# Ten instead of six low-rank merges in the last pair of a fused attention and FFN kernel, with weight parts staged in two more buffers

## The chip, the cores and the metric

The kernel runs on one core of one Trainium2 chip. Its time is the device time of one execution in microseconds (us), the median over runs of the same program: 644.33 us before the change (three runs, 643.79 to 645.38).

## The reference

Sixteen batches of 64 tokens with 1024 channels go through three residual stages. Cut to what matters:

```python
x = x + xattn(layernorm(x), ctx)      # fake_quant(x) @ fake_quant(ctx), ctx: (16, 1024, 1024)
x = x + attn(layernorm(x))            # qkv, rotary, causal softmax, 32 heads of 32, out projection
x = x + ffn(layernorm(x))

def ffn(x, W, bias, A, Bf, coeffs, scales):
    out = einsum('bsd,od->bso', x, W) + bias
    xa  = einsum('bsd,erd->ebsr', x, A)           # 16 adapters of rank 16
    return out + einsum('ebsr,eor,e->bso', xa, Bf, coeffs * scales)
```

Adapters are linear, so the kernel adds them into the weight once: W' = W.T + A.T @ (w * Bf), with the 16 adapters of rank 16 as one product of rank 256. All products are to be nearly as exact as in float32.

## The kernel before

Two batches make a pair of 128 token rows; there are eight pairs. The first two stages go pair by pair and leave each pair's rows in a scratch tensor in DRAM. The third stage (FFN) comes after all pairs, tile by tile of 128 rows, t = 0 to 7. A product in near float32 is three float16 products, high by high, high by low and low by high (`dense`, L1104 to L1106): ScalarE writes the high part of an operand and VectorE the low part, what is left after it.

The FFN's weight is built in 16 units of 128 x 512. For each unit u:

- `merge(u)` on PE: six matmuls of 128x512 into one of two PSUM banks (`cross` in the profile, L1281 to L1283). It waits for the sum of unit u-2, which frees its bank.
- `merged_sum(u)` on VectorE (L835): adds the bank to the unit of W.T, in place.
- `merged_high(u)` on ScalarE (L378), then `merged_low(u)` on VectorE (L840): the float16 parts, over weights of the attention stage that are no longer used.

Merges 0 to 7 lie among the matmuls of the last pair, 8 to 11 between that pair and the FFN, 12 to 15 in the first half of the FFN of tile 0. W.T arrives in five loads, into `raw` (units 0 to 3), `lnt` (4, 5) and the place `wt` over the query, key and value weights, which is free once the last pair has used them.

A tile of the FFN is: `stats3` (mean and reciprocal deviation on VectorE, 13 instructions, most of them of one element per row and each behind a wait for the one before), `apply3` (normalisation into `lnt`, L1018), `y_turn` (eight transposes on PE, L1095), `y_high` (ScalarE, L517), `y_low` (VectorE, L1030), two halves of 24 matmuls, and `y_evac` (L1039) into an output tile that `residual` (L1025) has filled with the input rows and the bias. SP loads the rows of tile t+2 when `residual(t)` is done (L650).

Every engine works through its own list in order, and waits on semaphores. There is no scheduler: order is what is written here, in tables such as `{5: [at(m, 0)]}`, which say behind which of the eight weight blocks of a product a step is issued. The names `merged_sum`, `merged_low`, `stats3` and so on stand in VectorE's list in `last_pair` and behind the loops.

Of the kernel before, what the change touches and what calls it, by code (L numbers as in the profile page):

```python
# [22 lines left out]
PAIRS = BATCH // 2  # L23
KC = DM // P
# [28 lines left out]
def build(nc, x, ctx_in, consts, consts16, scal, qkv_w, out_w, bias_rows, out_bias, ffn_wt, ffn_bias, lora_a, lora_b, lora_w, out):  # L53
# [6 lines left out]
    with es:  # L60
# [78 lines left out]
        wt_lnt = lnt[:, :].rearrange("p (u n) -> p u n", u=2)  # L139
        yn_h = [xn_h[:, :, :], q1v[:, 0:DM].rearrange("p (k t) -> p k t", k=KC)]  # L140
# [102 lines left out]
        def wt_unit(u):  # L243
            k, cols = merge_unit(u)
            if u < 4:
                return wt_early[:, u, :]
            return wt_lnt[:, u - 4, :] if u < 6 else wt[:, k, cols]

        wt_load = {0: 0, 4: 1, 6: 2, 8: 3, 12: 4}
# [31 lines left out]
        def _(act):  # L281
# [188 lines left out]
            def last_pair(i):  # L470
                for n in range(4):
                    lora_high(n)
                qk_evac(i, 0)
                qk_evac(i, 1)
                exponent(i, 0)
                exponent(i, 1)
                qk_evac(i, 2)
                p_evac(i, 0)
                p_evac(i, 1)
                qk_evac(i, 3)  # L480
                v_evac(i, 0)
                exponent(i, 2)
                exponent(i, 3)
                c_high(i, 0)
                p_evac(i, 2)
                v_evac(i, 1)
                p_evac(i, 3)
                c_high(i, 1)
                for u in range(6):
                    merged_high(u)  # L490
# [29 lines left out]
            for u in range(6, 2 * KC):  # L520
                merged_high(u)
# [7 lines left out]
        def _(sp):  # L529
# [85 lines left out]
            def load_wt(n):  # L615
                ks = (slice(0, 4), slice(4, 6), slice(6, 8), slice(0, 4), slice(4, 8))[n]
                cols = slice(0, NT) if n < 3 else slice(NT, DM)
                sp.dma_start((wt_early, wt_lnt)[n] if n < 2 else wt[:, ks, cols], wt_v[:, ks, cols]).then_inc(s_wt[n], 16)
# [11 lines left out]
            load_wt(1)  # L630
            sp.wait_ge(s_qkv, 6 * PAIRS)
            load_wt(2)
# [3 lines left out]
            load_wt(3)  # L636
# [49 lines left out]
        def _(dve):  # L686
# [144 lines left out]
            def merged_sum(u):  # L831
                dve.wait_ge(s_wf, u + 1)
                if u in wt_load:
                    dve.wait_ge(s_wt[wt_load[u]], 16)
                dve.scalar_tensor_tensor(wt_unit(u), X[u % 2][:, :], 1.0 / (WSC * WSC), wt_unit(u), ALU.mult, ALU.add).then_inc(s_wsum, 1)  # L835
# [94 lines left out]
            def last_pair(i):  # L930
                lora_weights()
                for n in range(4):
                    lora_low(n)
                rotate(i, 0)
                out_base(i)
                rotate(i, 1)
                merged_sum(0)
                merged_sum(1)
                softmax_in(i, 0)
                softmax_in(i, 1)  # L940
                rotate(i, 2)
                softmax_out(i, 0)
                softmax_out(i, 1)
                rotate(i, 3)
                merged_sum(2)
                merged_sum(3)
                softmax_in(i, 2)
                softmax_in(i, 3)
                merged_sum(4)
                softmax_out(i, 2)  # L950
                softmax_out(i, 3)
                merged_sum(5)
                c_low(i, 0)
                c_low(i, 1)

# [92 lines left out]
            merged_sum(6)  # L1048
            merged_sum(7)
            out_evac(PAIRS - 1, 0)  # L1050
            merged_low(6)
            merged_low(7)
            merged_sum(8)
            y_low(0, 0)
            merged_sum(9)
            merged_low(8)
            out_evac(PAIRS - 1, 1)
            merged(10, 11)
            residual(0, 0, 0)
            merged(12)  # L1060
            stats3(1, 0)
            merged(13, 14, 15)
            merged_low(2 * KC - 1)
            apply3(1, 1)
# [25 lines left out]
        def _(pe):  # L1090
# [287 lines left out]
            def next_pair(i, ahead):  # L1378
# [10 lines left out]
                def codes_turned(e):  # L1389
                    if ahead:  # L1390
# [4 lines left out]
                qkv(i, 1, {0: [at(c, 0)], 2: [at(c, 1)], 4: [at(codes_turned, 0), at(qk_turn, i, 0)], 5: [at(c, 2), at(m, 0)], 7: [at(c, 3)]})  # L1395
                qkv(i, 2, {1: [at(c, 4)], 3: [at(codes_turned, 1), at(qk_turn, i, 1)], 4: [at(c, 5), at(m, 1)], 6: [at(scores, i, 0)], 7: [at(c, 6)]})
                qkv(i, 3, {1: [at(c, 7)], 2: [at(m, 2)], 5: [at(turned, i, 0), at(qk_turn, i, 2)], 6: [at(turned, i, 2), at(p_turn, i, 0)], 7: [at(p_turn, i, 1)]})
                qkv(i, 4, {1: [at(m, 3)], 4: [at(evacuated, i, 1), at(qk_turn, i, 3)], 6: [at(c, 8)], 7: [at(c, 9)]})
                qkv(i, 5, {0: [at(scores, i, 1)], 1: [at(c, 10, 11), at(m, 4)], 2: [at(c, 12, 13), at(m, 5)], 3: [at(c, 14, 15), at(values_due, i, 0)], 4: [at(values, i, 0)],
                           6: [at(evacuated, i, 0), at(p_turn, i, 2)], 7: [at(p_turn, i, 3)]})  # L1400
                project(i, 0, 0, {2: [at(values_due, i, 1)], 3: [at(values, i, 1)]})
                project(i, 1, 0)
                if ahead:
                    x_turn(i + 1)
                else:
                    merge(6)
                    merge(7)
# [23 lines left out]
            for u in range(8, 12):  # L1431
                merge(u)

            def ffn(t, s, n, first=False):
# [8 lines left out]
                if first and n == 1:  # L1443
                    between = {4: [at(y_turn, 1)]}
# [65 lines left out]
```

## Time and profile before

| | |
|---|---|
| median of three runs | 644.33 us |
| the profiled execution | 645.53 us |
| its span | 643.9 us |
| PE busy | 604.1 us, 94% of the span |
| VectorE (DVE) busy | 448.6 us, 70% |
| ScalarE (ACT) busy | 297.6 us, 46% |
| DRAM traffic over the span | 169 GB/s |
| mean granted clock of PE | 0.986 of full |

The profile is of one execution. Its times count from the start of the span; what lies around the span is 1.6 us. PE is the matmul engine, DVE is VectorE, ACT is ScalarE, SPq the queue of transfers. A matmul is pipelined: the duration in its row runs past the start of the next one, so the rate is read from the starts.

### The profile page before, as it was taken

Reading aid. Unit: us, or ns where it says so; the run is one execution under the profiler, and the core shown is the slowest. Engines: PE = TensorE matmul, PEld = TensorE weight load, DVE = VectorE, ACT = ScalarE, POOL = GpSimd, SP = SyncE. Lnnn points to the kernel's source line nnn. Section 1 sums busy time; section 2 is a strip of 40 time slices with the busy share of each in tenths; the row PEclk is TensorE's granted clock in tenths of the full one; section 3 lists DMA queues with packets and bytes.
Section 4 is the critical chain, followed back from the end, with each engine's and each line's share of the span. In section 5 each row is a group of like instructions: output and inputs, shape, how many; then the busy total and the mean of one; then the engine's idle time right before and its main releaser. Section 6 shows DMA issues by size and latency. Waiting matters only on the chain.

```text
span 643.9 us, 12627 instructions
## 1 busy us (share of the span) xinstructions
PE 604.1 (94%) x4832; PEld 299.6 (47%) x4832; DVE 448.6 (70%) x897; ACT 297.6 (46%) x374; POOL 11.1 (2%) x20
## 2 busy tenths in 40 slices
PE   1669987999999999999999999999999999899997
PEld 0234442454545555554445455544544554354453
DVE  7599995779747854885586568537865569767661
ACT  5888765774455545545634554555331233101010
POOL 3000000000000000000000000000000000000000
PEclk9879999999999999999999999999999999899999
DMA  9999896862284156317712751463240062023221
GB/s 320 385 388 383 331 301 235 280 227 70 98 263 164 67 195 213 115 65 259 258 69 84 251 186 65 168 219 103 98 163 2 1 212 97 35 78 119 84 79 49
DMA packets 38878, 109.17 MB, mean 170 GB/s; under 512 B 4026, under 2 KB 4282, under 8 KB 38848
## 3 DMA queue, kind: packets, MB, share of 16 engines
q1 hardware_dynamic: 37072, 104.35, 46.3%
q0 software_dynamic: 1344, 4.23, 1.7%
q8 instruction: 20, 0.33, 0.2%
q10 hardware_dynamic: 432, 0.18, 0.1%
q14 instruction: 10, 0.08, 0.0%
HBM read 100.35 MB, written 8.39 MB: 169 GB/s over the span
## 4 chain that ended last, share of the span: by engine, by line
PE 81%; DVE 11%; DMA 3%; SPq 2%; ACT 1%; issue 1%; DVEq 0%; ACTq 0%
PE dense L1104 16%; PE dense L1106 15%; PE dense L1105 15%; PE cross L1141 7%; PE turn L1095 6%; DVE wq L774 4%; PE dense L1235 4%; PE dense L1236 4%; PE dense L1237 4%; PE score L1198 2%; SPq L532 2%; DMA wq<-in_ctx 2%; PE score L1222 2%; DMA lnt<-in_ctx 1%; PE dense L1117 1%
## 5 line engine op out<-in xcount | busy, mean ns | idle before, releaser
L1104 PE MATMUL dense<-wq,xn_h 128*128 128x512 f16 x400 | 152.4, 381 | 0.0
L1105 PE MATMUL dense<-wq,xn_h 128*128 128x512 f16 x400 | 151.9, 380 | 0.0
L1106 PE MATMUL dense<-wq,xn_l 128*128 128x512 f16 x400 | 151.9, 380 | 0.0
L318 ACT ACTIVATE code<-raw,cst,qc 128x1024 uint8<-128x1024 f32 x74 | 90.2, 1237 | 17.9 <-DMA raw<-in_ctx 17.1
L1141 PE MATMUL cross<-code,q1t 128*128 128x512 f16 x256 | 74.7, 393 | 8.5 <-ACT code L318 4.2
L1106 PEld LDWEIGHTS dense<-wq,xn_l 128*128 128x128 f16 x400 | 39.2, 98 | 47.5 <-issue 0.6
L1104 PEld LDWEIGHTS dense<-wq,xn_h 128*128 128x128 f16 x400 | 39.2, 98 | 40.8 <-issue 2.8
L1105 PEld LDWEIGHTS dense<-wq,xn_h 128*128 128x128 f16 x400 | 39.3, 98 | 37.8 <-issue 0.9
L334 ACT ACTIVATE at<-turn 128x512 f32<-128x512 f32 x32 | 19.1, 597 | 76.8 <-PE turn L1095 76.0
L318 ACT ACTIVATE code<-lnt,cst,qc 128x1024 uint8<-128x1024 f32 x34 | 42.1, 1238 | 26.9 <-DMA lnt<-in_ctx 19.9
L803 DVE TENSOR_REDUCE smx<-score 128x8 f32<-128x512 f32 x32 | 22.0, 686 | 44.0 <-PE score L1198 44.0
L791 DVE TENSOR_TENSOR rope<-dense,cst 128x512 f32<-128x512 f32 x32 | 22.0, 689 | 39.0 <-PE dense L1106 22.3
L1141 PEld LDWEIGHTS cross<-code,q1t 128*128 128x128 f16 x256 | 23.6, 100 | 44.8 <-ACT code L318 10.3
L1235 PE MATMUL dense<-wo,rope 128*128 128x512 f16 x112 | 42.5, 380 | 0.0
L1236 PE MATMUL dense<-wo,rope 128*128 128x512 f16 x112 | 42.4, 379 | 0.0
L1237 PE MATMUL dense<-wo,rope 128*128 128x512 f16 x112 | 42.4, 379 | 0.0
L342 ACT ACTIVATE at<-at 128x512 f32<-128x512 f32 x32 | 20.0, 626 | 34.8 <-DVE at L806 34.8
L348 ACT ACTIVATE at<-turn 128x512 f32<-128x512 f32 x32 | 19.0, 595 | 19.4 <-PE turn L1095 19.4
L780 DVE SCALAR_TENSOR_TENSOR xa<-cross,qc,xa 64x1024 f32<-64x1024 f32 x16 | 20.4, 1273 | 8.1 <-PE cross L1141 7.9
L1095 PE MATMUL turn<-cst,lnt 128*128 128x128 f32 x128 | 17.6, 283 | 7.9 <-DVE lnt L761 5.4
L829 DVE SCALAR_TENSOR_TENSOR xb<-dense,xb 128x512 f32<-128x512 f32 x16 | 11.0, 690 | 20.0 <-PE dense L1237 18.0
L1104 PE MATMUL dense<-wq,q1t 128*128 128x512 f16 x64 | 24.3, 379 | 0.0
(159 smaller groups left out, 935.8 us busy)
## 6 DMA issues: line engine op xcount, KB each, us to landing
raw<-in_ctx SPq DMA_DIRECT2D x74, 512.0 KB, 4.8
lnt<-in_ctx SPq DMA_DIRECT2D x34, 512.0 KB, 4.3
wo<-in_ctx SPq DMA_DIRECT2D x12, 512.0 KB, 9.1
wo<-in_qkv_w SPq DMA_DIRECT2D x12, 512.0 KB, 12.3
wq<-in_ctx SPq DMA_DIRECT2D x8, 512.0 KB, 11.5
wq<-in_qkv_w SPq DMA_DIRECT2D x8, 512.0 KB, 12.1
x_scratch<-xb SPq DMA_DIRECT2D x8, 512.0 KB, 3.2
wq<-x_scratch SPq DMA_DIRECT2D x8, 512.0 KB, 3.7
```

The source lines that it names most:

```text
L318: act.activation(low_bytes, src, ACT.Identity, scale=qc[:, 1:2], bias=z2).then_inc(s_u8, 1)
L774: dve.scalar_tensor_tensor(lo, staged(j), WSC, hi, ALU.mult, ALU.subtract).then_inc(s_wlo, 1)
L791: dve.tensor_tensor(t1, src, cosb, ALU.mult)
L803: link(dve.tensor_reduce(smx[:, g % 2, :], s3, AX.X, ALU.max))
L1095: ins = pe.transpose(bank[:, k * P:(k + 1) * P], src[:, c:c + P], ident)
L1104: pe.matmul(bank[:, :], a_h[:, k, :], w_hi, start=(k == 0 and not started), stop=False)
L1105: pe.matmul(bank[:, :], a_h[:, k, :], w_lo, start=False, stop=False)
L1106: ins = pe.matmul(bank[:, :], a_l[:, k, :], w_hi, start=False, stop=(k == KC - 1 and not last))
L1141: ins = pe.matmul(X[n][:, :], lhs, code[:, c % RING, n * NT:(n + 1) * NT], start=(kc == 0), stop=(kc == KC - 1))
L1235: pe.matmul(D[n][:, :], c_h[:, k, :], wo_h[:, k, cols], start=(k == 0), stop=False)
L1236: pe.matmul(D[n][:, :], c_h[:, k, :], wo_l[:, k, cols], start=False, stop=False)
L1237: ins = pe.matmul(D[n][:, :], c_l[:, k, :], wo_h[:, k, cols], start=False, stop=(k == KC - 1))
```

## The change

Merges 0 to 9 now lie in the last pair, 10 and 11 between it and the FFN, 12 to 15 as before. Units 6 and 7 of W.T are loaded into `xa` (the residual rows' buffer) and units 8 and 9 into the buffer of turned codes `q1t`, so both can arrive before the query, key and value weights are free; one load of six parts fills the rest. On VectorE the sums move up with their merges, the statistics and normalisation of the second tile go from between the sums to behind the last low part, and so do both residuals. On PE the second tile's transposes move from behind block 4 to behind block 7, the last, of the second half of tile 0.

```diff
+        wt_xa = xa[:, :].rearrange("p (u n) -> p u n", u=2)
+        wt_q1t = q1v.bitcast(F32).rearrange("p (u n) -> p u n", u=2)
...
-            return wt_lnt[:, u - 4, :] if u < 6 else wt[:, k, cols]
-        wt_load = {0: 0, 4: 1, 6: 2, 8: 3, 12: 4}
+            if u < 10:
+                return (wt_lnt, wt_xa, wt_q1t)[(u - 4) // 2][:, u % 2, :]
+            return wt[:, k, cols]
+        wt_load = {0: 0, 4: 1, 6: 2, 8: 3, 10: 4}
...
-                for u in range(6):
+                for u in range(10):
                     merged_high(u)
...
-                ks = (slice(0, 4), slice(4, 6), slice(6, 8), slice(0, 4), slice(4, 8))[n]
+                ks = (slice(0, 4), slice(4, 6), slice(6, 8), slice(0, 2), slice(2, 8))[n]
...
             load_wt(1)
+            load_wt(3)
+            sp.wait_ge(s_cp, PAIRS)
+            load_wt(2)
             sp.wait_ge(s_qkv, 6 * PAIRS)
-            load_wt(2)
             sp.wait_ge(s_st, 32)
             for n in range(2):
                 sp.dma_start(xs[n], x2_dram[n, :, :]).then_inc(s_x2[n], 16)
-            load_wt(3)
             load_wt(4)
...
                 rotate(i, 2)
+                merged_sum(2)
                 softmax_out(i, 0)
                 softmax_out(i, 1)
                 rotate(i, 3)
-                merged_sum(2)
                 merged_sum(3)
+                merged_sum(4)
+                merged_sum(5)
                 softmax_in(i, 2)
                 softmax_in(i, 3)
-                merged_sum(4)
+                merged_sum(6)
                 softmax_out(i, 2)
                 softmax_out(i, 3)
-                merged_sum(5)
+                merged_sum(7)
                 c_low(i, 0)
+                merged_sum(8)
                 c_low(i, 1)
+                merged_sum(9)
...
             apply3(0, 0)
-            merged_sum(6)
-            merged_sum(7)
+            merged_low(6)
             out_evac(PAIRS - 1, 0)
-            merged_low(6)
             merged_low(7)
-            merged_sum(8)
+            merged_low(8)
+            merged_low(9)
+            merged_sum(10)
             y_low(0, 0)
-            merged_sum(9)
-            merged_low(8)
+            merged_sum(11)
+            merged_low(10)
             out_evac(PAIRS - 1, 1)
-            merged(10, 11)
+            merged(12)
+            merged(13)
+            merged(14)
+            merged(15)
+            merged_low(2 * KC - 1)
+            stats3(1, 0)
+            apply3(1, 1)
             residual(0, 0, 0)
-            merged(12)
-            stats3(1, 0)
-            merged(13, 14, 15)
-            merged_low(2 * KC - 1)
-            apply3(1, 1)
             residual(1, 1, 0)
...
-                project(i, 0, 0, {2: [at(values_due, i, 1)], 3: [at(values, i, 1)]})
+                project(i, 0, 0, {0: [at(m, 8)], 2: [at(values_due, i, 1)], 3: [at(values, i, 1)]})
                 project(i, 1, 0)
...
-                    merge(6)
-                    merge(7)
+                    merge(9)
                 project(i, 0, 1)
                 project(i, 1, 1)
...
             y_turn(0)
-            for u in range(8, 12):
+            for u in range(10, 12):
                 merge(u)
...
-                    between = {4: [at(y_turn, 1)]}
+                    between = {7: [at(y_turn, 1)]}
```

What stands in a row now. VectorE at the end of the last pair, before: `lnt<-cross` is the sum of unit 5, `rope<-score` the low part of the attention result (`c_low`), `wq<-raw` low parts of weight units, `BN_STATS` the start of the first tile's statistics.

```order
L835 SCALAR_TENSOR_TENSOR lnt<-cross,lnt 128x512
L822 SCALAR_TENSOR_TENSOR rope<-score,rope 128x4x64 x4
L840 SCALAR_TENSOR_TENSOR wq<-raw,wq 128x512 x4
L697 BN_STATS st<-wq 128x6
L698 BN_STATS st<-wq 128x6
```

VectorE at the same place in the changed kernel: `xa<-cross` is the sum of unit 7, `q1t<-cross` are those of units 8 and 9.

```order
L840 SCALAR_TENSOR_TENSOR xa<-cross,xa 128x512
L827 SCALAR_TENSOR_TENSOR rope<-score,rope 128x4x64 x2
L840 SCALAR_TENSOR_TENSOR q1t<-cross,q1t 128x512
L827 SCALAR_TENSOR_TENSOR rope<-score,rope 128x4x64 x2
L840 SCALAR_TENSOR_TENSOR q1t<-cross,q1t 128x512
L845 SCALAR_TENSOR_TENSOR wq<-raw,wq 128x512 x4
L702 BN_STATS st<-wq 128x6
L703 BN_STATS st<-wq 128x6
```

A sum now stands between the two `c_low`, and one between the second of them and the first low part of a weight, where none was.

PE at the end of tile 0's FFN, before: `dense` are its matmuls, `turn<-cst,lnt` the second tile's transposes.

```order
L1106 MATMUL dense<-wq,xn_l 128x512
L1104 MATMUL dense<-wq,xn_h 128x512
L1105 MATMUL dense<-wq,xn_h 128x512
L1106 MATMUL dense<-wq,xn_l 128x512
L1095 MATMUL turn<-cst,lnt 128x128 x8
L1104 MATMUL dense<-wq,xn_h 128x512
L1105 MATMUL dense<-wq,xn_h 128x512
L1106 MATMUL dense<-wq,xn_l 128x512
```

PE there in the changed kernel: the `dense<-wq,q1t` behind the transposes are the second tile's own first matmuls.

```order
L1116 MATMUL dense<-wq,xn_l 128x512
L1114 MATMUL dense<-wq,xn_h 128x512
L1115 MATMUL dense<-wq,xn_h 128x512
L1116 MATMUL dense<-wq,xn_l 128x512
L1105 MATMUL turn<-cst,lnt 128x128 x8
L1114 MATMUL dense<-wq,q1t 128x512
L1115 MATMUL dense<-wq,q1t 128x512
L1116 MATMUL dense<-wq,q1t 128x512
```

The transposes had three weight blocks (nine matmuls) of tile 0 behind them and now have those of the second tile, which need the transposed rows.

VectorE around the second tile's statistics, before: `wq<-cross` is a sum, `wq<-wq` a low part, `xa<-wq` the first residual.

```order
L840 SCALAR_TENSOR_TENSOR wq<-wq 128x512
L1025 TENSOR_TENSOR xa<-wq 128x1024
L835 SCALAR_TENSOR_TENSOR wq<-cross,wq 128x512
L840 SCALAR_TENSOR_TENSOR wq<-wq 128x512
L697 BN_STATS st<-wq 128x6
L698 BN_STATS st<-wq 128x6
```

VectorE at the last sums in the changed kernel.

```order
L840 SCALAR_TENSOR_TENSOR wq<-cross,wq 128x512
L845 SCALAR_TENSOR_TENSOR wq<-wq 128x512
L840 SCALAR_TENSOR_TENSOR wq<-cross,wq 128x512
L845 SCALAR_TENSOR_TENSOR wq<-wq 128x512 x2
L702 BN_STATS st<-wq 128x6
L703 BN_STATS st<-wq 128x6
```

The statistics now come behind the last of the low parts, and the first residual behind the normalisation.

## Rows read from the trace of the kernel before

**Rows 1.** The page: busy time of engines, and granted clock in 40 slices.
```profile
PE 604.1 (94%) x4832; PEld 299.6 (47%) x4832; DVE 448.6 (70%) x897; ACT 297.6 (46%) x374; POOL 11.1 (2%) x20
...
PEclk9879999999999999999999999999999999899999
```

**Rows 2.** Stretches: window, length, busy us by engine, granted clock, DMA share, GB/s.
```profile
534.00:550.00 16.00, 13.57 (x66) 6.12 (x63) 14.34 (x32) 5.27 (x9) 0.00 (x0) 1.00 0.18 67
550.00:557.00 7.00, 6.27 (x22) 2.55 (x23) 6.28 (x10) 1.89 (x3) 0.00 (x0) 0.76 0.00 0
```

**Rows 3.** Waits of PE, 534 to 557 us: total, times, longest.
```profile
PE cross L1281 <- DVE wq L835: 3.2, 3, 2.2
```

**Rows 4.** Timeline of PE: start, duration, instruction, [idle before, releaser].
```profile
538.76 0.39 PE L1281 MATMUL cross<-code 128*128 128x512 f16 x1 [0.60 <-DVE wq L835]
...
540.55 0.39 PE L1281 MATMUL cross<-code 128*128 128x512 f16 x1 [0.33 <-DVE wq L835]
...
550.73 0.39 PE L1281 MATMUL cross<-code 128*128 128x512 f16 x1 [2.23 <-DVE wq L835]
...
551.17 0.60 PE L1283 MATMUL cross<-code 128*128 128x512 f16 x1
...
554.80 0.38 PE L1106 MATMUL dense<-wq,xn_l 128*128 128x512 f16 x1
```

**Rows 5.** Timeline of PE, around the transposes of the last stage's rows.
```profile
529.36 0.38 PE L1235 MATMUL dense<-wo,rope 128*128 128x512 f16 x1
...
534.53 1.04 PE L1095 MATMUL turn<-cst,lnt 128*128 128x128 f32 x8
...
559.55 1.04 PE L1095 MATMUL turn<-cst,lnt 128*128 128x128 f32 x8
...
562.36 0.38 PE L1104 MATMUL dense<-wq,q1t 128*128 128x512 f16 x1
```

**Rows 6.** Timeline of VectorE, then of PE, in the last pair's attention.
```profile
500.42 0.69 DVE L814 TENSOR_TENSOR at<-at,ssum 128x512 f32<-128x512 f32 x1
...
501.86 0.60 PE L1095 MATMUL turn<-cst,at 128*128 128x128 f32 x4
```

**Rows 7.** Timeline of VectorE, 524 to 566 us.
```profile
524.68 0.76 DVE L822 SCALAR_TENSOR_TENSOR rope<-score,rope 128x256 f16<-128x256 f32 x2 [5.08 <-ACT rope L354]
525.48 2.50 DVE L840 SCALAR_TENSOR_TENSOR wq<-raw,wq 128x512 f16<-128x512 f32 x4
...
532.93 0.81 DVE L1018 TENSOR_SCALAR lnt<-wq,mv,nw 128x1024 f32<-128x1024 f32 x1
...
546.35 0.69 DVE L697 BATCH_NORM_STATS2 st<-wq 128x6 f32<-128x512 f32 x1
...
549.98 0.69 DVE L835 SCALAR_TENSOR_TENSOR wq<-cross,wq 128x512 f32<-128x512 f32 x1
...
553.09 0.69 DVE L835 SCALAR_TENSOR_TENSOR wq<-cross,wq 128x512 f32<-128x512 f32 x1 [0.62 <-PE cross L1283]
...
555.09 0.81 DVE L1018 TENSOR_SCALAR lnt<-wq,mv,nw 128x1024 f32<-128x1024 f32 x1
555.81 1.22 DVE L1025 TENSOR_TENSOR outb<-wq 128x1024 f32<-128x1024 f32 x1
...
560.81 1.29 DVE L1030 TENSOR_TENSOR q1t<-turn,q1t 128x512 f16<-128x512 f32 x2 [3.19 <-ACT q1t L517]
562.02 0.68 DVE L697 BATCH_NORM_STATS2 st<-wq 128x6 f32<-128x512 f32 x1
...
565.95 0.81 DVE L1018 TENSOR_SCALAR lnt<-wq,mv,nw 128x1024 f32<-128x1024 f32 x1
```

**Rows 8.** Timeline of PE, near the start.
```profile
24.17 2.51 PE L1141 MATMUL cross<-code,q1t 128*128 128x512 f16 x10 [3.52 <-DVE xa L781]
```

**Rows 9.** SP's queue: the load of the third rows; landing times of its line.
```profile
545.41 0.34 SPq L650 DMA_DIRECT2D wq<-x_scratch  x1
...
DMA to landing us min/median/max: 3.2/3.5/3.7
```

More of the change, by code:

```diff
@@ L519, in _ @@
             y_high(0, 0)
-            for u in range(6, 2 * KC):
+            for u in range(10, 2 * KC):
                 merged_high(u)
@@ L615, in load_wt @@
             def load_wt(n):
-                ks = (slice(0, 4), slice(4, 6), slice(6, 8), slice(0, 4), slice(4, 8))[n]
+                ks = (slice(0, 4), slice(4, 6), slice(6, 8), slice(0, 2), slice(2, 8))[n]
                 cols = slice(0, NT) if n < 3 else slice(NT, DM)
-                sp.dma_start((wt_early, wt_lnt)[n] if n < 2 else wt[:, ks, cols], wt_v[:, ks, cols]).then_inc(s_wt[n], 16)
+                sp.dma_start((wt_early, wt_lnt, wt_xa, wt_q1t)[n] if n < 4 else wt[:, ks, cols], wt_v[:, ks, cols]).then_inc(s_wt[n], 16)
             for j in range(2):
@@ L1394, in next_pair @@
                 qkv(i, 0, {5: [at(next_codes, i + 1)]} if ahead else {})
-                qkv(i, 1, {0: [at(c, 0)], 2: [at(c, 1)], 4: [at(codes_turned, 0), at(qk_turn, i, 0)], 5: [at(c, 2), at(m, 0)], 7: [at(c, 3)]})
-                qkv(i, 2, {1: [at(c, 4)], 3: [at(codes_turned, 1), at(qk_turn, i, 1)], 4: [at(c, 5), at(m, 1)], 6: [at(scores, i, 0)], 7: [at(c, 6)]})
+                qkv(i, 1, {0: [at(c, 0)], 2: [at(c, 1)], 4: [at(codes_turned, 0), at(qk_turn, i, 0)], 5: [at(c, 2), at(m, 0)], 7: [at(c, 3), at(m, 1)]})
+                qkv(i, 2, {1: [at(c, 4)], 3: [at(codes_turned, 1), at(qk_turn, i, 1)], 4: [at(c, 5)], 6: [at(scores, i, 0)], 7: [at(c, 6)]})
                 qkv(i, 3, {1: [at(c, 7)], 2: [at(m, 2)], 5: [at(turned, i, 0), at(qk_turn, i, 2)], 6: [at(turned, i, 2), at(p_turn, i, 0)], 7: [at(p_turn, i, 1)]})
-                qkv(i, 4, {1: [at(m, 3)], 4: [at(evacuated, i, 1), at(qk_turn, i, 3)], 6: [at(c, 8)], 7: [at(c, 9)]})
-                qkv(i, 5, {0: [at(scores, i, 1)], 1: [at(c, 10, 11), at(m, 4)], 2: [at(c, 12, 13), at(m, 5)], 3: [at(c, 14, 15), at(values_due, i, 0)], 4: [at(values, i, 0)],
-                           6: [at(evacuated, i, 0), at(p_turn, i, 2)], 7: [at(p_turn, i, 3)]})
-                project(i, 0, 0, {2: [at(values_due, i, 1)], 3: [at(values, i, 1)]})
+                qkv(i, 4, {0: [at(m, 3)], 3: [at(m, 4)], 4: [at(evacuated, i, 1), at(qk_turn, i, 3)], 6: [at(c, 8), at(m, 5)], 7: [at(c, 9)]})
+                qkv(i, 5, {0: [at(scores, i, 1)], 1: [at(c, 10, 11)], 2: [at(c, 12, 13), at(m, 6)], 3: [at(c, 14, 15), at(values_due, i, 0)], 4: [at(values, i, 0)],
+                           5: [at(m, 7)], 6: [at(evacuated, i, 0), at(p_turn, i, 2)], 7: [at(p_turn, i, 3)]})
+                project(i, 0, 0, {0: [at(m, 8)], 2: [at(values_due, i, 1)], 3: [at(values, i, 1)]})
                 project(i, 1, 0)
```

## The prediction

> **What bounds the kernel now.** I read the page first: PE is busy for 94% of the span, and the clock row dips only near the start and in the slice that begins at 547 us [rows 1]. A change that adds and removes no matmul can therefore give back only waits and slow matmuls. The stretches show where they are: PE idles 2.43 us from 534 to 550 us, and from 550 to 557 its granted clock is 0.76 [rows 2]. All waits of that stretch are of a merge for the VectorE sum two merges earlier [rows 3]. PE's own timeline gives their price [rows 4]. A matmul's row lasts 0.38 us but its successor starts 0.2155 us later (24 matmuls from 529.36 to 534.53 [rows 5]), so a wait costs 0.165 more than the idle time named: 0.765 at 538.76, 0.495 at 540.55, 2.395 at 550.73, together 3.65 us. The third one has the thirteen statistics steps of the second rows before it: VectorE is in them from 546.35 to 549.98 [rows 7]. After it the matmuls from 551.17 to 554.80 take 0.42 us apart: the granted clock is at half, 1.2 GHz. Nine of them in 3.63 us instead of 1.94 cost 1.69. So 5.35 us is all that this junction can give. Everything behind 562.36, where the second rows' FFN starts, is matmuls without a gap.
>
> VectorE's rows overlap likewise, by 0.09: the one of 0.81 at 555.09 is followed at 555.81 [rows 7]. So a sum, a low part or an evacuation of 0.69 takes 0.60 in a row, a normalisation 0.72, a residual of 1.22 takes 1.13.
>
> Two margins of before decide the rest. The first rows' transposes start at 534.53, and the normalised rows were ready at 532.93 + 0.81 = 533.74 [rows 5, 7]: 0.79 us to spare. The second rows' FFN starts at 562.36 and its low parts were ready at 560.81 + 1.29 = 562.10 [rows 5, 7]: 0.26 to spare. The change touches both.
>
> **Inside the last pair.** Two merges (six matmuls each, 1.293 us) come into it: everything after the fourth merge is up to 2.59 us later than before, with no new matmul in total. VectorE does each sum in a hole that it has. The narrowest place is the second transpose of the probabilities: before, its data were ready at 500.42 + 0.69 = 501.11 and it started at 501.86 [rows 6]; with one sum (0.60) in front it is ready at 501.71. I cost all of this at nothing. The new buffers change no instruction's shape, and their loads are issued while the first sums are made, six merges or more before their use. The last load, now 1.5 MB for six parts, belongs to merges that come 10 us after the old ones; also nothing.
>
> **The first rows, where the change breaks down.** Before, VectorE starts the last low part of the attention result at 524.68, is through at 525.48, and needs 7.45 us to the start of the normalisation at 532.93: four low parts of weights, the statistics, two more low parts [rows 7]. Now one merge more stands ahead of the second values (one of two already in the shift), so these come 2.59 + 1.29 = 3.88 later and VectorE is through at 529.36. But its next instruction is now the sum of the tenth merge, and that merge stands on PE between the first and second half of the projection. Before, the second half started at 529.36 [rows 5]; now at 529.36 + 2.59 = 531.95, just behind the merge. VectorE gets a merge's end 0.2 us after the next matmul begins (0.38 modelled less 0.2155, and 0.04 to release), so it sits from 529.36 to about 532.14, in order, with four low parts, the statistics and the normalisation queued behind. Then: sum 0.60, chain 7.45, so the normalisation starts at 540.19 and ends at 541.00. PE is free for the transposes at 534.53 + 2.59 = 537.12 and starts them at 541.04: **a wait of 3.92 us**. Nothing else stands ahead of it on PE; the two merges left come behind it.
>
> **The first FFN.** From 540.19 VectorE needs 0.72 to its next instruction, then four low parts and one projection evacuation at 0.60 each, the sum of the eleventh merge at 0.60, and the low part of the transposed rows, 1.29 to its end [rows 7]: 545.80. PE has transposes of 0.87 (1.04 less 0.165 [rows 5]) and two merges: free at 541.04 + 0.87 + 2.59 = 544.50, it starts at 545.84: **a wait of 1.34**. Before, four merges covered this. The merges inside the FFN's first half no longer wait: between two of them VectorE has a sum and a low part to do, 1.2 us (1.8 with an evacuation), and a merge with the FFN's three matmuls gives it 1.94. So the old 3.65 and the old 1.69 are gained in full.
>
> **The second rows.** The last merge's last matmul starts 35 matmuls after 545.84, at 553.38, its sum at 553.80. From sum to the end of the last low part is 2.00 (553.09 to 555.09), so the statistics start at 555.80, take 3.63, the normalisation starts at 559.43; 0.72 later the first residual, then the second, the first output evacuation, and at 563.01 the low part of the second rows, whose end is 1.29 later: 564.30 [rows 7]. PE does 72 matmuls from 545.84 (15.52), ends at 561.36, transposes until 562.23, and starts the second FFN at 564.34: **a wait of 2.11**. Even an idle VectorE would leave most of it: before, transposes at 559.55 led to low parts at 562.10, 2.55 us, of which PE fills 0.87 [rows 5, 7]. The transposes used to have three weight blocks (1.94 us) behind them and now have none.
>
> Up to here: 3.92 + 1.34 + 2.11 = 7.37 of new waits against 5.35, and the FFN starts at 564.34 against 562.36, +2.0. One more term: SP asks for the third rows when the first residual is done, before at 545.41 [rows 9], now at about 561.55, and such a load takes 3.2 to 3.7 us [rows 9]. VectorE wants them at 564.22 and has them at 564.8 to 565.2. From there to the next normalisation's end is 4.74 (562.02 to 565.95 + 0.81), against PE's 5.17 + 0.04: 0.2 to 0.5 late at the next transposes, and 0.1 at the FFN behind. I take 0.4. Sum at full clock: **+2.4 us**.
>
> **The clock.** A 2.23 us wait was followed by the slow stretch, waits of 0.60 and 0.33 were not; but a wait of 3.52 at 24.17 was followed by ten matmuls in 2.51, full speed [rows 4, 8]. So a slow stretch of 3.63 us behind each long new wait may come or not: between nothing and, for the first, transposes of 1.76 and then 4.4 slow matmuls, by which the eleventh merge ends 1.3 later, and with it its sum and the low part behind that (+1.3); for the second 1.69, less the 0.4 of lateness it hides (+1.3). The rows show one long wait of each kind; I take the first in full, its wait being well over 2.23, and half of the second, at 2.11 near it: +1.3 and +0.6.
> The Trainium skill (TensorE: Matmul & The Clock Gate, section HAM oscillation) warns that each idle gap that is long enough returns PE to half clock, and that this is paid again at every gap. [...]
>
> **The sum.** 2.4 + 1.3 + 0.6 = 4.3 us on the profiled execution, 645.53 (its span is 643.9 and 1.6 lie around it), so 649.8. That execution was 1.2 over the median 644.33, which gives 648.6. Its own range is +2.0 (last term nil, no slow stretch) to +5.0 (both in full): 646.3 to 649.3.
>
> **The rivals.**
> 1. The plan works and the time falls. For it: every wait of rows 3 is a merge behind a sum, the statistics leave the path between merges, and the merges stop waiting. It needs the normalised first rows by 537.12, and the second rows' low parts as soon as their transposes allow. Against it: VectorE is in order, and the sum of the tenth merge cannot start before 532.1. If both chains were somehow short enough, only the 1.7 us behind the moved transposes would remain: 5.35 - 1.7 = 3.65 off, 640.7. Chance 0.07.
> 2. VectorE does not lose its 2.78 us (sums that wait less than the order says, or low parts that overlap more). Then the first wait is 1.14, and the others 1.34 and 2.11, too short for a slow stretch apart from the last: 4.59 + 0.4 - 5.35 = -0.4, with half a stretch +0.2: 644 to 645, no change. Chance 0.14.
> 3. Both slow stretches come in full: 649.3 by the sum above, or neither: 646.7. These belong to my case, 0.79 in all.
> 4. Did the change not move what it says? The order rows show that it does.
>
> **How the numbers follow.** 0.3% (1.9 us), about what a measurement can tell from no change, is just under the case's lower end; I leave 0.02 of it there. Slower 0.77, same 0.16, faster 0.07. For eight in ten the range reaches from 645.0, into the second rival, to 650.0.
>
> **What would show it.** In the profile of the changed kernel: transposes of the third-stage rows waiting for the normalisation for 3 to 4 us near 541, with VectorE idle near 530 until a merge ends; dense matmuls waiting about 1.3 us near 546 and about 2 us near 564 for low parts; no merge waiting for a sum; a slow stretch behind the first. If PE's transposes start by 538, or VectorE passes the tenth sum before 530.5, the first step is wrong; if the second FFN starts within 0.5 us of the transposes' end, the third is. If the total is within 1.9 us of before, the waits were over-counted.

## The result, and the profile after

| | before | changed |
|---|---|---|
| median, 8 runs each | 645.48 us | 650.28 us |
| lowest and highest | 643.79 to 647.00 | 648.17 to 651.55 |
| ratio | | 1.0071, 95% interval 1.0052 to 1.0090 |
| profiled execution, its span | 645.53, 643.9 us | 650.28, 648.6 us |

The change makes the kernel 0.7% slower: 4.6 us by the ratio, 4.8 by the medians. Forecast were +4.3 us and 648.6; the way and the size of the change hold, but 650.28 lies above the range's end of 650.0. (The kernel before had a median of 644.33 in its first three runs, 645.48 in eight, 645.07 in 31 runs beside the experiments e1, e4, e5 and e6, and 645.70 in eleven beside e2, e3, e7 and e8. Each ratio below is taken against the runs beside it.)

One word on the title: eight merges lay on PE in the last pair before, as the description says, and two come into it. Six is the number of their sums that VectorE had in its list of the last pair; now it has ten there.

The page's lines that answer to [rows 1]. PE has 606.3 us of busy time instead of 604.1, with the same 4832 matmuls.

```profile
span 648.6 us, 12628 instructions
...
PE 606.3 (93%) x4832; PEld 302.0 (47%) x4832; DVE 449.1 (69%) x897; ACT 298.3 (46%) x374; POOL 11.1 (2%) x20
...
PEclk9879988999999999999999999999999998999999
```

The waits of PE from 480 us to the end, as in [rows 3] total, times and longest. No merge waits for a sum any more; the three waits that are left are all new.

```profile
PE turn L1105 <- DVE lnt L1027: 3.8, 1, 3.8
PE dense L1114 <- DVE q1t L1039: 2.0, 1, 2.0
PE dense L1114 <- DVE xn_l L1039: 0.7, 1, 0.7
```

The stretches of the changed kernel, with the columns of [rows 2]:

```profile
537.40:542.50 5.10, 1.32 (x7) 0.42 (x5) 4.60 (x16) 0.00 (x0) 0.00 (x0) 0.97 0.00 0
542.50:549.00 6.50, 5.81 (x24) 3.25 (x25) 5.53 (x10) 1.92 (x4) 0.00 (x0) 0.76 0.00 0
549.00:567.00 18.00, 16.03 (x79) 7.69 (x78) 14.96 (x30) 4.14 (x7) 0.00 (x0) 1.00 0.17 62
```

PE works 1.32 of 5.10 us in the first and has a clock of 0.76 in the second; VectorE is busy 4.60 of the 5.10 and the DMA engines are idle: PE waits for VectorE's list, not for data from outside.

PE's timeline there, the counterpart of [rows 4, 5]:

```profile
542.47 1.97 PE L1105 MATMUL turn<-cst,lnt 128*128 128x128 f32 x8 [3.78 <-DVE lnt L1027]
544.23 0.63 PE L1291 MATMUL cross<-code 128*128 128x512 f16 x1
544.66 0.63 PE L1292 MATMUL cross<-code 128*128 128x512 f16 x1
...
545.76 0.38 PE L1292 MATMUL cross<-spare,code 128*128 128x512 f16 x1
...
548.33 0.39 PE L1114 MATMUL dense<-wq,xn_h 128*128 128x512 f16 x1 [0.69 <-DVE xn_l L1039]
...
563.88 1.04 PE L1105 MATMUL turn<-cst,lnt 128*128 128x128 f32 x8
566.89 0.39 PE L1114 MATMUL dense<-wq,q1t 128*128 128x512 f16 x1 [1.97 <-DVE q1t L1039]
```

The transposes take 1.97 us instead of 1.04 and the first merge's matmuls are 0.43 apart: half clock, 1.2 GHz. The row at 545.76 is the first at full clock again. Then VectorE's timeline, the counterpart of [rows 7]:

```profile
529.97 0.76 DVE L827 SCALAR_TENSOR_TENSOR rope<-score,rope 128x256 f16<-128x256 f32 x2 [2.46 <-ACT rope L358]
533.55 0.69 DVE L840 SCALAR_TENSOR_TENSOR q1t<-cross,q1t 128x512 f32<-128x512 f32 x1 [2.82 <-PE cross L1293]
534.16 2.49 DVE L845 SCALAR_TENSOR_TENSOR wq<-raw,wq 128x512 f16<-128x512 f32 x4
536.56 0.68 DVE L702 BATCH_NORM_STATS2 st<-wq 128x6 f32<-128x512 f32 x1
...
541.60 0.81 DVE L1027 TENSOR_SCALAR lnt<-wq,mv,nw 128x1024 f32<-128x1024 f32 x1
...
546.39 0.69 DVE L840 SCALAR_TENSOR_TENSOR wq<-cross,wq 128x512 f32<-128x512 f32 x1 [0.97 <-PE cross L1293]
547.00 1.28 DVE L1039 TENSOR_TENSOR xn_l<-turn,xn_h 128x512 f16<-128x512 f32 x2
...
558.31 0.69 DVE L702 BATCH_NORM_STATS2 st<-wq 128x6 f32<-128x512 f32 x1
...
561.95 0.81 DVE L1027 TENSOR_SCALAR lnt<-wq,mv,nw 128x1024 f32<-128x1024 f32 x1
562.68 1.22 DVE L1034 TENSOR_TENSOR xa<-wq 128x1024 f32<-128x1024 f32 x1
563.82 1.22 DVE L1034 TENSOR_TENSOR outb<-wq 128x1024 f32<-128x1024 f32 x1
564.95 0.68 DVE L1048 SCALAR_TENSOR_TENSOR xa<-dense,xa 128x512 f32<-128x512 f32 x1
565.55 1.28 DVE L1039 TENSOR_TENSOR q1t<-turn,q1t 128x512 f16<-128x512 f32 x2
567.27 0.69 DVE L702 BATCH_NORM_STATS2 st<-wq 128x6 f32<-128x512 f32 x1 [0.44 <-DMA wq<-x_scratch]
```

To be seen: after the last `c_low` (529.97) VectorE stands for 2.82 us in front of the sum of unit 9; the chain from 534.16 to 541.60 follows; then from 558.31 statistics, normalisation, two residuals, an evacuation and only then the low parts of the second rows, each behind the other without a hole.

### The profile page after: what moved, and what is told of

It is laid out like the page before. It is cut to its first block, busy times and chain, and to the rows that moved or that the text cites. A ratio compares the mean times of both kernels' runs of the same rounds, so it can differ in the third digit from the quotient of the medians.

```text
span 648.6 us, 12628 instructions
## 1 busy us (share of the span) xinstructions
PE 606.3 (93%) x4832; PEld 302.0 (47%) x4832; DVE 449.1 (69%) x897; ACT 298.3 (46%) x374; POOL 11.1 (2%) x20
## 4 chain that ended last, share of the span: by engine, by line
PE 82%; DVE 10%; DMA 3%; SPq 2%; issue 2%; ACT 1%; DVEq 0%; ACTq 0%
PE dense L1114 16%; PE dense L1116 15%; PE dense L1115 15%; PE cross L1151 7%; PE turn L1105 7%; PE dense L1245 4%; PE dense L1246 3%; PE dense L1247 3%; DVE wq L779 2%; PE score L1208 2%; SPq L536 2%; DMA wq<-in_ctx 2%; PE score L1232 2%; PE dense L1261 1%; PE dense L1329 1%
## 5 line engine op out<-in xcount | busy, mean ns | idle before, releaser
L1105 PE MATMUL turn<-cst,lnt 128*128 128x128 f32 x128 | 19.5, 302 | 13.4 <-DVE lnt L766 6.0
L1105 PEld LDWEIGHTS turn<-cst,lnt 128*128 128x128 f32 x128 | 16.7, 156 | 18.1 <-DVE lnt L766 6.5
```

The lines of the kernel that those rows point to most:

```text
L1105: ins = pe.transpose(bank[:, k * P:(k + 1) * P], src[:, c:c + P], ident)
```

## What the executions have in common

The two kernels do the same until the last pair, yet the time until then is different each time. So I measure from a mark, the first of the eight transposes in front of the last pair's products (466.82 in the first profile of before), to the first and to the second rows' FFN, and from there to the end of the span. The junction is the stretch between the last pair's last matmul and the second rows' FFN; slow matmuls are those at half clock. Each row is one profiled execution, in us:

| kernel | mark at | mark to 1st FFN | mark to 2nd FFN | from there to the end | slow matmuls, in the junction or just behind it |
|---|---|---|---|---|---|
| before (first profile) | 466.82 | 75.04 | 95.54 | 81.51 | behind the 2.2 wait |
| before (f1) | 467.09 | 75.04 | 93.85 | 81.51 | none |
| before (f2) | 466.31 | 75.04 | 93.85 | 81.51 | none |
| changed (first profile) | 468.22 | 80.11 | 98.67 | 81.71 | behind the 3.8 wait |
| changed (e8) | 468.54 | 80.23 | 98.78 | 81.59 | behind the 3.8 wait |
| changed (g1) | 468.68 | 80.28 | 98.82 | 81.84 | behind the 3.8 wait |
| changed (g2) | 466.51 | 80.05 | 98.60 | 81.75 | behind the 3.8 wait |
| e1, sum behind | 466.74 | 76.26 | 94.80 | 83.18 | behind the 2.0 wait |
| e4, first wait filled | 468.27 | 79.04 | 97.58 | 83.17 | behind the 2.0 wait |
| e7, all three filled | 467.65 | 79.05 | 97.60 | 82.05 | none |
| e2, transposes at block 4 | 466.44 | 79.67 | 98.22 | 83.19 | behind the 3.8 wait |
| e3, and small residuals | 467.30 | 80.76 | 98.12 | 82.43 | behind the 3.8 wait |
| e5, statistics alone | 466.56 | 75.03 | 92.43 | 81.52 | none |
| e6, reordered | 467.25 | 74.03 | 91.57 | 81.48 | none |

## The experiments

**e1, the sum of the tenth merge moved.** Does VectorE's stand in front of that sum hold up the first rows?

```diff
                 c_low(i, 1)
-                merged_sum(9)
...
             apply3(0, 0)
+            merged_sum(9)
             merged_low(6)
```

> The changed kernel with one VectorE instruction moved: the sum of the tenth merge goes from the end of the last pair to behind the normalisation of the first rows. My theory (VectorE stands 2.8 us in front of that sum, and the first rows' transposes wait for what is queued behind it): the 3.8 us wait in front of those transposes falls to about 0.5 us, the slow stretch behind it goes too, the wait for the first rows' low parts grows to about 1.9 us because the sum is now in front of them, the wait of 2.0 at the second rows stays. Together 4 us less than the changed kernel, so 646 to 647, ratio to the kernel before 1.000 to 1.002. Rival (more merges in the last pair or the new buffers cost time by themselves, the waits are only where it shows): the time stays at that of the changed kernel, ratio 1.006 to 1.008.

Measured: 646.39 (12 runs), ratio to before 1.0019 (1.0003 to 1.0034). PE's timeline:

```profile
537.60 1.09 PE L1105 MATMUL turn<-cst,lnt 128*128 128x128 f32 x8 [0.39 <-DVE lnt L1026]
...
543.00 0.39 PE L1114 MATMUL dense<-wq,xn_h 128*128 128x512 f16 x1 [1.72 <-DVE xn_l L1038]
...
561.54 0.39 PE L1114 MATMUL dense<-wq,q1t 128*128 128x512 f16 x1 [1.96 <-DVE q1t L1038]
...
562.00 0.63 PE L1116 MATMUL dense<-wq,q1t 128*128 128x512 f16 x1
...
564.56 0.63 PE L1116 MATMUL dense<-wq,q1t 128*128 128x512 f16 x1
```

The first wait is 0.39 instead of 3.78, the second grew to 1.72, as said; the second FFN starts 3.9 us earlier after the mark than in the changed kernel. One instruction's place is worth most of the loss: without slow matmuls in either, the first FFN starts 2.8 us earlier than in e4 below (76.26 against 79.04 after the mark), and 2.82 is what VectorE stood idle. What was not foreseen: the slow matmuls now follow the third wait (562.00 to 564.56) and take 1.5 back, so from the mark to the end only 2.4 us are gained. The total of 646.39 agrees with the forecast of 646 to 647 in part by luck: the profiled execution, 646.40, had its mark 1.5 us earlier than the changed kernel's first profile, and only 2.4 us of the difference lie behind the mark.

**e4, the first wait filled** with matmuls that nothing reads.

```diff
+            for n in range(16):
+                pe.matmul(S[0][:, :], wo_h[:, 0, 0:P], wo_h[:, 1, 0:NT], start=True, stop=True)
             y_turn(0)
```

> The changed kernel with 16 matmuls of 128x512 (3.45 us at full clock) added on PE directly in front of the first rows' transposes, into a score bank that nothing reads any more. They do no work of the reference. My theory of the clock (half clock follows PE's long wait, and costs 1.3 us of the result): the 3.8 us wait shrinks to about 0.4, no slow matmul follows, the transposes start at the same time as in the changed kernel, and the total is about 1.3 us less than the changed kernel, ratio to the kernel before 1.005. Rival (the slow stretch costs nothing, since VectorE's chain sets the FFN's start anyway): no change, ratio 1.007. A third: VectorE is not the one waited for, then the added 3.45 us are paid, ratio 1.012.

Measured: 648.83 (8 runs), 1.0061 (1.0041 to 1.0082).

```profile
542.51 1.09 PE L1105 MATMUL turn<-cst,lnt 128*128 128x128 f32 x8 [0.32 <-DVE lnt L1027]
...
547.31 0.39 PE L1114 MATMUL dense<-wq,xn_h 128*128 128x512 f16 x1 [1.12 <-DVE xn_l L1039]
...
565.85 0.39 PE L1114 MATMUL dense<-wq,q1t 128*128 128x512 f16 x1 [1.95 <-DVE q1t L1039]
...
566.31 0.63 PE L1116 MATMUL dense<-wq,q1t 128*128 128x512 f16 x1
...
568.87 0.63 PE L1116 MATMUL dense<-wq,q1t 128*128 128x512 f16 x1
```

The added 3.45 us cost nothing, the transposes run at full clock and the second FFN starts 1.1 us earlier after the mark: of the 1.3 that the slow stretch behind the first wait was to cost, 1.1 is seen. But another came behind the third wait (the time from the second FFN to the end is 83.17 instead of 81.7), and the total shows little of it. The forecast of 1.005 and the rival's 1.007 both lie in the interval, so it is the trace that decides between them, not the time.

**e7, all three waits filled** (16, 3 and 8 matmuls: the 16 of e4, and those below in front of the waits for the low parts).

```diff
                 if n == 0:
+                    if isinstance(t, int) and t < 2:
+                        for _ in range(8 if t else 3):
+                            pe.matmul(S[0][:, :], wo_h[:, 0, 0:P], wo_h[:, 1, 0:NT], start=True, stop=True)
                     pe.wait_ge(s_yl, 2 * t + 2)
```

> The changed kernel with matmuls that nothing reads in all three new waits of PE: 16 in front of the first rows' transposes, 3 in front of the first FFN, 8 in front of the second. In the kernel with only the first 16 the slow stretch was seen behind the second rows' wait instead. My theory (half clock follows whichever long wait of PE the chip takes, and costs 1.3 to 1.7 us wherever it falls): with all three filled there is no slow stretch from the last pair on, the start of the second FFN stays, and the time from the last pair to the end is 1.3 us or more below that of the kernel with the first wait filled; ratio to the kernel before 1.003 to 1.004. Rival (slow stretches come at random, whatever PE does): one is still seen, ratio 1.006.

Measured: 649.44 (6 runs), 1.0062 (1.0044 to 1.0080). The waits of PE from 480 us on:

```profile
PE dense L1114 <- DVE xn_l L1039: 0.6, 2, 0.5
PE turn L1105 <- DVE lnt L1027: 0.3, 1, 0.3
PE dense L1114 <- DVE q1t L1039: 0.2, 1, 0.2
```

No slow matmul is left in the junction, the second FFN starts at 97.60 as with one wait filled, and the end comes 1.1 us earlier than there. 97.60 against 93.85 for before without slow matmuls is 3.75: this is the pure difference of the waits, 3.72 by the prediction's terms (7.37 - 3.65). The ratio of 1.003 to 1.004 was missed, and so, by a little, was the gain of 1.3. From the mark to the end it is 179.65, which is 2.6 us above before with its slow stretch and 4.3 above before without it; the forecast of the ratio had assumed the first every time, the measured 1.0062 is 4.0. This is one profile: an execution without a slow stretch is also what a stretch that comes at random would give now and then, so that the filling removed it is likely, not shown.

**e2 and e3, the transposes of the second rows behind block 4 again**, in e3 with the first two tiles' residuals cut short.

```diff
-                    between = {7: [at(y_turn, 1)]}
+                    between = {4: [at(y_turn, 1)]}
```
```diff
-                dve.tensor_tensor(yo[s], xs[s], fbias, ALU.add).then_inc(s_y0, 1)
+                n = 16 if isinstance(t, int) and t < 2 else DM
+                dve.tensor_tensor(yo[s][:, 0:n], xs[s][:, 0:n], fbias[:, 0:n], ALU.add).then_inc(s_y0, 1)
```

> The changed kernel with the second rows' transposes back behind block 4 of the first rows' second half; all else as changed. My theory (their low parts cannot come earlier, because on VectorE the statistics, the normalisation, both residuals and an output evacuation stand in front of them): the 2.0 us wait of the second FFN is split, 0.9 in front of the transposes and 1.2 in front of the FFN, and the FFN starts when it did; ratio to the changed kernel 0.999 to 1.001. Rival (the late place of the transposes costs the wait): the second FFN starts 1.9 us earlier, ratio to the changed kernel 0.997.

> As the kernel with the transposes behind block 4, and the residuals of the first two tiles add only 16 of 1024 columns (the other columns of these two tiles are left without input rows and bias), so 2.0 us of VectorE go from in front of the second rows' low parts. My theory (VectorE's work sets the second FFN): 0.9 us of wait in front of the transposes stays, the wait of the FFN goes, and it starts about 1.2 us earlier than in the changed kernel; ratio to it 0.998. With the transposes' place as the cause: the same as the kernel without small residuals. If both are bound by something else: no change.

Measured: e2 649.17 (6 runs), 1.0057 (1.0040 to 1.0075); e3 649.16, 1.0058 (1.0039 to 1.0077). PE in e2:

```profile
560.59 1.10 PE L1105 MATMUL turn<-cst,lnt 128*128 128x128 f32 x8 [0.71 <-DVE lnt L1027]
...
564.66 0.39 PE L1114 MATMUL dense<-wq,q1t 128*128 128x512 f16 x1 [1.03 <-DVE q1t L1039]
```

In e2 the one wait of 1.97 has become two, 0.71 and 1.03. The second FFN starts 0.5 earlier after the mark, not 1.9, and even this 0.5 was there at the first FFN, through the clock: from the first FFN's start to the second's it is 18.55 us in e2 and 18.56 in the changed kernel. VectorE's chain sets the second FFN, not the place of the transposes. The time from there to the end is 1.5 longer than in the changed kernel, because VectorE's next residual waited 4.02 us for an output store to land, where it waits 2.6 in the other profiles; PE then waits 1.44 us at 577.61 for the low parts behind it:

```profile
574.45 1.23 DVE L1034 TENSOR_TENSOR xa<-wq 128x1024 f32<-128x1024 f32 x1 [4.02 <-DMA result<-xa]
```

In e3 the wait in front of the second FFN is gone, and from the first FFN's start to the second's it is 17.36 us, 1.2 less than in e2, as expected. So VectorE's work in front of those low parts is what the second FFN waits for. The totals cannot tell e3 from e2, nor either from the changed kernel: in the profile of e3 the slow stretch lasts past 546, which holds up the first FFN by 0.65 us against the changed kernel, and PE waits 0.54 for the third rows' normalisation. What the shorter residuals are worth in the whole time is not shown.

**e5, one part alone:** the kernel before with the second rows' statistics behind the last merge.

```diff
-            merged(12)
-            stats3(1, 0)
-            merged(13, 14, 15)
+            merged(12, 13, 14, 15)
             merged_low(2 * KC - 1)
+            stats3(1, 0)
             apply3(1, 1)
```

> The kernel before with one part of the change alone: the statistics of the second rows go behind the last merge and the last low part; six merges in the last pair, transposes of the second rows behind block 4, residuals where they were. My theory (this part is a gain, the ten merges and the late transposes are the loss): the 2.4 us wait of the last merge and the slow stretch behind it (1.7) go, the second rows' transposes wait 0.9 for their normalisation and their FFN starts when VectorE is through, at about 559.3 instead of 562.4: 3 us less, ratio 0.995. Rival (the statistics are only moved in front of another wait of the same size, VectorE being full here): ratio 0.999 to 1.001.

Measured: 642.60 (12 runs), 0.9961 (0.9942 to 0.9980).

```profile
538.50 0.39 PE L1280 MATMUL cross<-code 128*128 128x512 f16 x1 [0.60 <-DVE wq L835]
...
540.29 0.39 PE L1280 MATMUL cross<-code 128*128 128x512 f16 x1 [0.32 <-DVE wq L835]
...
556.06 1.09 PE L1094 MATMUL turn<-cst,lnt 128*128 128x128 f32 x8 [0.71 <-DVE lnt L1018]
```

The 2.23 wait is gone and 0.71 stands in front of the transposes. Against before with its slow stretch the second FFN starts 3.1 us earlier, as expected, against before without it 1.4; the median lies between. This part of the change is a gain. The forecast ratio of 0.995 lies in the interval.

**e6, ten merges and the new buffers, with VectorE's list laid out anew:**

```diff
                 merged_sum(8)
+                stats3(0, 0)
                 c_low(i, 1)
-                merged_sum(9)
...
-            for u in range(4):
-                merged_low(u)
-            stats3(0, 0)
             merged_low(4)
             merged_low(5)
             apply3(0, 0)
+            for u in range(4):
+                merged_low(u)
+            merged_sum(9)
             merged_low(6)
+            merged_low(7)
             out_evac(PAIRS - 1, 0)
-            merged_low(7)
+            dve.wait_ge(s_wfl, 8)
+            residual(0, 0, 0)
+            y_low(0, 0)
+            merged_sum(10)
+            merged_sum(11)
             merged_low(8)
             merged_low(9)
-            merged_sum(10)
-            y_low(0, 0)
-            merged_sum(11)
             merged_low(10)
...
             merged(14)
+            residual(1, 1, 0)
             merged(15)
             merged_low(2 * KC - 1)
             stats3(1, 0)
             apply3(1, 1)
-            residual(0, 0, 0)
-            residual(1, 1, 0)
...
-                    between = {7: [at(y_turn, 1)]}
+                    between = {5: [at(y_turn, 1)]}
```

> Ten merges in the last pair and the new buffers as in the changed kernel, but VectorE's list is laid out anew: statistics of the first rows in the idle time in front of the second low part of the attention result, low parts 4 and 5 ahead of 0 to 3, normalisation of the first rows directly behind them, sum of the tenth merge behind that, first residual ahead of the first rows' low parts, second residual ahead of the last sum, statistics of the second rows behind the last low part, second rows' transposes behind block 5, bias loaded ahead of the last weight parts. My theory (the waits come from VectorE's order and its total work, not from the number of merges in the pair): first rows' transposes and FFN start without a wait, second FFN waits at most 1 us, its start is at about 557.6 on the scale of the kernel before (562.4): 4.8 us less than the kernel before, ratio 0.9925. Rival (VectorE is simply full, no order helps): within 0.2% of the kernel before.

Measured: 641.97 (12 runs), 0.9957 (0.9939 to 0.9974), the fastest here, faster than both kernels; against e5 it cannot be told apart by the intervals.

```profile
537.56 1.04 PE L1106 MATMUL turn<-cst,lnt 128*128 128x128 f32 x8
...
556.15 1.09 PE L1106 MATMUL turn<-cst,lnt 128*128 128x128 f32 x8 [0.22 <-DVE lnt L1027]
...
558.82 0.39 PE L1115 MATMUL dense<-wq,q1t 128*128 128x512 f16 x1 [0.28 <-DVE q1t L1039]
```

Of PE's idle time 0.22 and 0.28 are left. This is with ten merges in the pair and the same buffers as the changed kernel, so neither of them costs time by itself: the first rows' transposes start 70.31 us after the mark, 67.71 in the kernel before, and the difference is just the two merges. At the second FFN the gain is 4.0 us against before with its slow stretch (4.8 were forecast) and 2.3 without. The forecast ratio of 0.9925 was missed and lies outside the interval. The layout changes several places at once, and what each is worth was not measured; nor do the ten merges gain anything that can be told from e5, which has the old places.

**e8, and f1, f2, g1, g2: both kernels again,** unaltered, to find why executions of one kernel differ by 4 us.

> The changed kernel again, unaltered, beside its variants: ratio to the kernel before 1.007, the three waits as in its first profile (3.8, 0.7, 2.0). Whether the slow stretch is behind the first wait, behind the third or behind both is open; both would make the time from the last pair to the end 1.3 us longer than in the first profile.

> The kernel before, profiled again. Asked: where the last pair's transposes start (466.82 in its first profile, 468.22 and 468.54 in the two of the changed kernel), and how long it is from there to the end (177.06 against 180.4). My theory: everything up to that mark is the same work in both kernels, and its place moves by 1 to 2 us from execution to execution with the slow stretches of the first 115 us; so marks of both kernels overlap, between 466.3 and 468.6, while the time from the mark to the end is 177.1 within 0.5 unless the slow stretch of the last merge is missing (then 175.4). Rival: the changed kernel is slower in its first part too, and the marks of before stay below 467.

> The changed kernel, profiled again: by my theory the mark lies anywhere from 466.3 to 468.6 and the time from it to the end is 180.4 with one slow stretch and 181.7 with two. By the rival the mark is above 468 every time.

> As for the first repeated profile of the kernel before: mark between 466.3 and 468.6, 177.1 from it to the end.

> As for the first repeated profile of the changed kernel: mark between 466.3 and 468.6, 180.4 or 181.7 from it to the end.

Measured: e8 650.50 (6 runs), 1.0070 (1.0051 to 1.0089); single executions f1 644.13, f2 643.32, g1 650.99, g2 648.51. The marks overlap (466.31 to 467.09 and 466.51 to 468.68): the rival, which wanted all marks of the changed kernel above 468, is refuted by g2, and by e1 and e2 (466.74 and 466.44), whose first part is that of the changed kernel. Three of its own four do lie above those of before. Over all profiles, the ten kernels with the changed first part have their mark at 467.6 on average and the four with the first part of before (e5 with them) at 466.7; whether a difference of the first part is behind that, or chance, stays open. The surprise is the junction. In f1, behind the same wait as in [rows 4]:

```profile
550.99 0.39 PE L1281 MATMUL cross<-code 128*128 128x512 f16 x1 [2.22 <-DVE wq L835]
551.22 0.38 PE L1282 MATMUL cross<-code 128*128 128x512 f16 x1
551.43 0.38 PE L1283 MATMUL cross<-code 128*128 128x512 f16 x1
551.65 0.38 PE L1281 MATMUL cross<-spare,code 128*128 128x512 f16 x1
```

The matmuls behind it are 0.22 us apart, full clock. In two of three profiles of before there is no slow stretch here, and it is 1.7 us shorter. In all four of the changed kernel there is one behind the 3.8 wait.

## Why the prediction was wrong, point by point

- **Last pair, nothing.** Right: no wait of PE there, and e6 keeps ten merges and the buffers at no cost.
- **First rows, 3.92.** Measured 3.78 + 0.165 = 3.95, from the cause named: VectorE idle 2.82 (2.78 forecast) in front of the tenth sum. e1 shows the cause by moving it.
- **First FFN, 1.34.** Measured without slow matmuls (e4) 1.12 + 0.165 = 1.29; with them 0.86, since the slow transposes and merges fill the wait.
- **Second rows, 2.11.** Measured 1.97 + 0.165 = 2.14. That VectorE's chain and not only the late transposes sets it: e2 and e3.
- **Lateness at the third rows, 0.4.** Measured 0.1 to 0.3 over 81.51 in the changed kernel's profiles, 0.54 in e7: VectorE waits 0.44 for the load (567.27).
- **The clock behind the first wait, 1.3.** Nearly right: 98.60 to 98.82 against 97.58 and 97.60 in e4 and e7, 1.0 to 1.2. (The prediction's working says that the eleventh merge ends 1.3 later; by its own terms it ends 1.8 later, 0.9 in the transposes and 0.9 in 4.4 slow matmuls, and 0.5 of it is covered because VectorE is not there yet.) **Behind the third, half of 1.3, 0.6.** Not seen in any of four profiles of the changed kernel; seen in e1 and e4, where the first wait had none.
- **The row at 24.17**, which stood for "no slow stretch behind a long wait", was one execution. f1 and f2 have the same wait of 3.52 us in the same place, and from 24 to 28 us the granted clock is 1.00 in the first profile, 0.60 in f1 and 0.50 in f2. PE's timeline in f1, then in f2, where the sixteen matmuls are 0.4 us apart:

```profile
24.19 4.45 PE L1141 MATMUL cross<-code,q1t 128*128 128x512 f16 x12 [3.52 <-DVE xa L781]
24.17 6.39 PE L1141 MATMUL cross<-code,q1t 128*128 128x512 f16 x16 [3.52 <-DVE xa L781]
```

- **The step that failed** is the last one of the sum: "That execution was 1.2 over the median 644.33, which gives 648.6". The median of three runs was no anchor for that. In the eight runs of the comparison the kernel before has 645.48, so the profiled execution of 645.53 was 0.05 over it, not 1.2. This term alone is 1.15 of the 1.68 us by which 650.28 misses 648.6, and without it the sum's 649.8 lies inside the range. The runs of before go from 642.74 to 647.47, and the range had no room for that. The other 0.5 is the change itself, +4.8 by the medians against +4.3.
- **That +4.3 came so near is partly luck.** On the costs it is 1.0 too high (the half stretch of 0.6, and 0.1 to 0.3 each at the first stretch and the third rows): from the mark to the end the changed kernel's first profile is 3.3 us longer than the first profile of before, where +4.3 was forecast. The two whole executions are 4.75 apart because 1.4 more lie ahead of the mark, where the change is not. On the gain it is too hopeful: "So the old 3.65 and the old 1.69 are gained in full" takes the 1.69 as if every execution had it, and it is there in one of three. Against an execution without it the change costs 180.4 - 175.4 = 5.0 us; over the three profiles of before and the four of the changed kernel the mean difference is 4.5. The two errors cancel. The slow stretch may also be a part of the 1.2 that was taken off, and then the same microseconds were counted twice; this was not shown, since what lies ahead of the mark varies by as much.
- **Rivals.** That VectorE would not lose its 2.78 us, or that the time falls, is refuted by the 2.82 in the trace and by the ratio.

## What to carry to other kernels

Moving a step earlier on one engine moves its partner's wait into the other engine's ordered list: before doing so, ask what is queued behind that wait and who needs it; here, with one sum in front of a 7.4 us chain, PE waited 3.95 us, and 0.56 with the sum moved (e1), while all the stalls that the change removed came to 3.65. Where two changes come together, cost them apart: the statistics alone were a gain of 0.4%. Before a wait's after-effects are booked as a gain, look at more than one execution, and count from a mark that lies just ahead of the change. And where a kernel's runs are 4 us apart, as here, a median of three can be more than 1 us off: forecast the change, and give the absolute time the width of the runs.

## What the runs showed of the hardware

Half clock after a wait of PE is no fixed price. Behind the 3.8 us wait it came in six of six profiles (the changed kernel's four, e2, e3). Behind the 2.2 us wait it came in one of three, and behind the 2.0 us wait in two of six; in both of these the earlier long wait had been shortened (e1) or filled (e4). Behind the same wait of 3.52 us near the start one execution of before ran ten matmuls at full clock and the other two ran at half clock at once or from the fourth matmul on (24.89). With one wait filled with idle matmuls the slow stretch was seen at a later one (e4), with all three filled there was none (e7), in one profile each.

The Trainium skill (TensorE: Matmul & The Clock Gate, section HAM oscillation) has PE return to half clock at every gap that is long enough. For the 3.8 us waits the traces agree; for those of 2.0, 2.2 and 3.52 they show it only in some executions.

The mean granted clock of an execution goes with its time, loosely: of the 31 runs of before the nine at 0.989 took 643.9 us on average and the eight at 0.981 or less 646.7, but those at 0.986 go from 642.91 to 646.44. It does not tell where the slow stretches were: the first profile of before and f2 both have 0.986, and only the first has one in the junction.
